# A sixteen-group, four-layer pipeline: order strings for all engines, a bank table, and step vectors with stationary weights

## The reference

```
x = x + L0(_gn(x))   # routed 1x1, 3x3, 1x1 convolutions; weights mixed from 8 experts per sample
x = x + L1(_gn(x))   # in-projection, depthwise conv, selective scan over permuted tokens, out-projection
x = x + L2(_gn(x))   # 1x1, 3x3 offsets, deformable 3x3, 1x1
x = x + L3(_gn(x))   # three convolutions, each squared (y + 1)^2, with batch norm
```

```
x_h = _gather_last(xf, perm)                    # tokens in the order of a permutation per head
dbc = einsum('oc,bcn->bon', dbc_w, xf) + dbc_b  # "step vectors": dt, B, C per head and token
dt = softplus(dbc[:, :, 0])
h = exp(dt*A) * h + (dt*B) * x ; y = C . h + D*x  # scan over the 196 tokens
y = _gather_last(y, inverse of perm)
```

## Time and profile before

| | us |
|---|---|
| median of three runs (1036.54 to 1048.52) | 1043.89 |
| the profiled execution | 1048.19 |
| its span, first to last instruction | 1046.0 |
| TensorE busy | 935.8 |
| VectorE busy | 731.9 |
| ScalarE busy | 550.1 |
| GpSimd busy | 362.4 |

### The profile page before, as it was taken

The page is one execution under the profiler, slowest core; times in us unless marked ns, Lnnn a source line. Parts: engine busy times, 40 slices in busy tenths (PEclk is TensorE's granted clock), DMA queues, the critical chain, the costliest instruction groups (busy, mean ns, idle before and its releaser), DMA issues.

```text
span 1046.0 us, 19785 instructions
## 1 busy us (share of the span) xinstructions
PE 935.8 (89%) x7460; PEld 635.9 (61%) x7460; DVE 731.9 (70%) x2047; ACT 550.1 (53%) x1155; POOL 362.4 (35%) x320
## 2 busy tenths in 40 slices
PE   3788988999999899999999999999999998887766
PEld 2555656666666566666666666666666665646454
DVE  2567377786878587878878687878787868756332
ACT  1143353756556474748475655657474747361412
POOL 3013433435251625344342525152524343342200
PEclk9889999999999999999999999999999999889998
DMA  9101153352626253544536262626353444426060
GB/s 220 37 8 44 40 141 121 85 177 75 184 75 178 70 169 108 145 128 116 161 94 188 76 190 72 182 79 168 96 164 113 128 130 118 147 64 189 15 207 16
DMA packets 116547, 123.33 MB, mean 118 GB/s; under 512 B 64802, under 2 KB 99750, under 8 KB 116454
## 3 DMA queue, kind: packets, MB, share of 16 engines
q1 hardware_dynamic: 107812, 105.45, 34.6%
q0 software_dynamic: 6144, 13.71, 4.6%
q10 hardware_dynamic: 2498, 2.91, 1.2%
HBM read 84.31 MB, written 37.73 MB: 117 GB/s over the span
## 4 chain that ended last, share of the span: by engine, by line
PE 30%; DVE 24%; issue 17%; POOL 13%; ACT 9%; DMA 5%; SPq 1%; ACTq 0%; POOLq 0%; DVEq 0%
PE ps L625 27%; DVE c_w L1301 4%; ACT y L986 3%; POOL rs L1215 3%; POOL b_ex L1215 3%; POOL b_cr L1215 2%; POOL b_yp L1263 2%; ACT L986 2%; POOL b_res L1215 2%; DVE y L1306 2%; DVE x L1309 2%; DVE st L1336 2%; DMA b_yp<-y_turned,b_to 2%; DVE b_xf L1309 1%; DVE y L1309 1%
## 5 line engine op out<-in xcount | busy, mean ns | idle before, releaser
L1263 POOL DMA_INDIRECT b_yp<-y_turned,b_to x64 | 90.3, 1411 | 271.5 <-DMA y_turned<-b_yt 256.9
L625 PE MATMUL ps<-y,inw 128*128 128x392 f32 x384 | 140.2, 509 | 1.3 <-DVE y L1306 1.3
L1215 POOL TENSOR_TENSOR rs<-ve,root 128x4 f32<-128x4 f32 x64 | 66.1, 1032 | 200.9 <-DVE ve L1305 200.4
L1336 DVE BATCH_NORM_STATS2 st<-x 128x6 f32<-128x196 f32 x256 | 73.7, 350 | 88.0 <-POOL x L1215 76.0
L1301 DVE TENSOR_TENSOR c_w<-c_w,c_hat 126x1176 f32<-126x1176 f32 (+1 forms) x64 | 97.8, 1580 | 11.2 <-DMA c_w<-hat_turned 11.2
L625 PE MATMUL ps<-c_w,c_zt 126*64 126x196 f32 x896 | 88.7, 345 | 11.6 <-DVE c_w L1301 6.9
L625 PEld LDWEIGHTS ps<-y,inw 128*128 128x128 f32 x384 | 70.6, 194 | 46.4 <-issue 6.8
L625 PE MATMUL ps<-w,a_S 128*32 128x384 f32 (+2 forms) x1280 | 81.6, 392 | 7.5 <-DVE a_S L1309 5.7
L625 PE MATMUL ps<-c 128*128 128x256 f32 (+1 forms) x284 | 86.7, 442 | 0.0
L986 ACT ACT_TABLE_LOAD x50 | 64.2, 1283 | 37.5 <-PE ps L625 36.7
L625 PEld LDWEIGHTS ps<-c_w,c_zt 126*64 126x64 f32 x896 | 63.8, 142 | 31.8 <-issue 14.3
(11 more groups left out here) (203 smaller groups left out, 2025.3 us busy)
## 6 DMA issues: line engine op xcount, KB each, us to landing
c_w<-hat_turned SPq DMA_DIRECT2D x32, 771.8 KB
c_w<-hat_turned SPq DMA_DIRECT2D x32, 578.8 KB
z_turned<-c_z SPq DMA_DIRECT2D x32, 441.0 KB
c_zt<-z_turned SPq DMA_DIRECT2D x16, 882.0 KB
b_xp<-x_turned SPq DMA_DIRECT2D x32, 222.0 KB
x<-in_x SPq DMA_DIRECT2D x32, 196.0 KB, 2.7
y_turned<-b_yt SPq DMA_DIRECT2D x32, 196.0 KB
out<-x SPq DMA_DIRECT2D x32, 196.0 KB, 7.3
```

The costliest lines, as they stand in the source:

```text
L625: return nc.tensor.matmul(o, l, r, start=start, stop=stop)
L1215: return nc.gpsimd.tensor_tensor(out=o, in0=x, in1=y, op=op)
L1263: nc.gpsimd.indirect_dma_start(out=YP[:, m, h].rearrange("p b d -> p (b d)"), out_offset=None, in_=y_dram[g % 2], in_offset=bass.IndirectO ...
L1336: last = nc.vector.bn_stats(st[s][:, 2 * c + b, :], x[:, c, b, :])
```

## The change

1. **Order.** `PLAN` and `FROM` go. `ORDER` has a string per engine with a letter per step (`LETTERS` names the stages); the steps of a stage come in their own order. Period by period, the order of the steady loop on TensorE differs from the old one in where steps stand, and the first four and last three groups have orders of their own.
2. **SyncE.** Per period in the loop: the two stores of `c_hat`, the first two hat loads, the two stores of `c_z`, the two stores of `y`, the load of `c_zt`, the second two hat loads, the load of `x_turned`, the output. Before: stores of `c_hat`, stores of `c_z`, first two hat loads, `c_zt`, one second hat load, stores of `y`, the other one, output, `x_turned`. The second pair of inputs is loaded ahead of the constants.
3. **Banks.** `BANKS` names the bank of each take; every step takes its bank ahead of its waits for data.
4. **Fillers.** `keep_busy` goes. `BUSY` gives the number of 128-column products (`group` times `group`) put between the wait for the bank and the wait for data: 7 ahead of `c1` and 4 ahead of `off` in groups 3 to 12, 13 and 4 in group 13, and 348 others in 48 places of the first six and last four groups, 14 of them ahead of the first routing product.
5. **Step vectors.** `dbcw` (34 columns, padded to 64) are the weights and `b_xf` streams, 196 columns a product. ScalarE adds the bias in the eviction to `b_row`, TensorE transposes `b_row` in two halves, VectorE evicts both into `XT`. The transposes of `b_xf` are taken for both samples in one bank, evicted by ScalarE (first token half) and VectorE (second). `b_bc`, `xq` as a tensor and its addition go; `xq` is a view of the reloaded block. Two small parameter loads are added (`dbcb`).

```diff
-        self.turn[f, g] = len(self.turn)
+        bank = int(self.banks[len(self.turn)])
+        self.turn[f, g] = bank, self.uses[bank]
+        self.uses[bank] += 1
...
+        ("off", 12): 4, ("c1", 13): 13, ("n1", 15): 3, ("off", 13): 4, ("n3", 12): 5, ("d2", 12): 6,
+        (("pt", 0), 14): 14, (("pt", 1), 14): 12, ("d1", 13): 7, (("pt", 0), 15): 5, (("pt", 1), 15): 3,
+        (("out", 0), 15): 6, ("n2", 15): 16, ("acc", 14): 2, ("off", 15): 9, ("n3", 14): 13,
+        ("d1", 14): 13, ("d2", 14): 7, ("acc", 15): 3, ("n3", 15): 13, ("d1", 15): 13, ("d2", 15): 7}
...
+LETTERS = "acbstuofgdhkz"
+ORDER = {
+    "tensor": (
...
+        "uussscktttddtkocoackoodddddfcdgcgcgcguguuuuuucggggggbcuchsssuussscktttddtkocoackoodddddfcdgcgcgcgugu"
...
+    "sync": (
+        "kaggddgguudddttkaggddgguudddttkaggddgguudddttkaggddgguudddttkaggddgguudddttkaggddgguudddttkggddgguud"
...
+BANKS = (
+        "0123456021345602134560213456021345602134560231456032145601435260143526014352601435206153240513420634"
...
+    return [next(todo[letter]) for letter in ORDER[name]]
...
+                t = ring.tile(f, g)
+                for _ in range(BUSY.get((f, g), 0)):
+                    mm(t[:, 0:128], k128("group"), k128("group"))
+                return t
...
-            def keep_busy(f, g, n):
-
-                t = take(f, g)
-                if first(g):
-                    pe.wait_ge(ld_c, 16 * 2)
-                lo = at128["expand"][0]
-                for _ in range(n):
-                    mm(t[:, 0:2 * N], ident, c128[:, lo:lo + 2 * N])
-
-            def take_early(f, g, ring=R):
-
-
-                t = take(f, g, ring)
-                for _ in range(BUSY.get((f, g), 0)):
-                    mm(t[:, 0:256], ident, c128[:, 0:256])
...
-                k, tt, b = part, part // G, part % G
-                if k == 0:
-                    pe.wait_ge(b_xf_ok.sem, b_xf_ok.count(g))
+                if i == 0:
+                    tt = part
+                    t = take(("xt", tt), g)
+                    if tt == 0:
+                        pe.wait_ge(b_xf_ok.sem, b_xf_ok.count(g))
+                        if first(g):
+                            pe.wait_ge(ld_c, 16 * 2)
+                    for h in range(HEADS):
+                        for b in range(G):
+                            last = nc.tensor.transpose(t[0:HT, (h * G + b) * HD:(h * G + b + 1) * HD],
+                                                       b_xf[:, h, b, tt * HT:(tt + 1) * HT], ident)
+                    last.then_inc(R.filled(("xt", tt), g), 1)
+                if i == 1:
                     if first(g):
-                        pe.wait_ge(ld_c, 16 * 2)
-                t = take(("xt", k), g)
-                cols = slice(tt * HT, (tt + 1) * HT)
-                for h in range(HEADS):
-                    nc.tensor.transpose(t[0:HT, h * XD:h * XD + HD], b_xf[:, h, b, cols], ident)
-                o = t[0:HT, 0:HEADS * XD].rearrange("p (h x) -> p h x", h=HEADS)[:, :, HD:XD]
-                for c in range(CC):
-                    last = mm(o, b_xf[:, c, b, cols], dbcw[:, c, :, :], start=(c == 0), stop=(c == CC - 1))
-                last.then_inc(R.filled(("xt", k), g), 1)
+                        pe.wait_ge(zeros, NZERO)
+                    t = take("db", g)
+                    for c in range(CC):
+                        for b in range(G):
+                            last = mm(t[half(b), 0:N], dbcw[:, c, :], b_xf[:, c, b, :], start=(c == 0), stop=(c == CC - 1))
+                    last.then_inc(R.filled("db", g), 1)
+                if i == 3:
+                    t = take("rows", g)
+                    drained(pe, "db", g)
+                    for tt in range(2):
+                        last = nc.tensor.transpose(t[0:HT, tt * 128:(tt + 1) * 128], b_row[:, tt * HT:(tt + 1) * HT], ident)
+                    last.then_inc(R.filled("rows", g), 1)
...
-                    keep_busy("c1", g, 1)
                 if i == 1:
...
-                if i == 2 and part == 0:
-                    keep_busy("off", g, 2)
-                if i == 2 and part == 1:
+                if i == 2:
+                    take("off", g)
...
+                if i == 0:
+                    if g:
+                        act.wait_ge(*x_out.at(g - 1))
+                    filled(act, ("xt", 0), g)
+                    fn(XT[:, 0, :, :, 0:HD].rearrange("p h b x -> p (h b) x"), R.tile(("xt", 0), g)[0:HT, :]
+                       .rearrange("p (q x) -> p q x", x=HD), ACT.Copy).then_inc(R.drained(("xt", 0), g), 1)
+                if i == 2:
+                    if first(g):
+                        act.wait_ge(ld_d, 16 * 13)
+                    filled(act, "db", g)
+                    fn(b_row[:, :], R.tile("db", g)[:, 0:N], ACT.Identity, bias=dbcb[:, 0:1])\
+                        .then_inc(R.drained("db", g), 1)
...
-                        pool.wait_ge(b_xq_ok.sem, b_xq_ok.count(g))
+                        pool.wait_ge(*x_back.at(g))
...
-                    tt(xq[:, :, :], XP[:, :, :, :, HD:XD].rearrange("p t h b x -> p (t h b) x"), b_bc[:, :, :], ALU.add)\
-                        .then_inc(b_xq_ok.sem, 1)
+                    filled(v, "rows", g)
+                    for tt in range(2):
+                        last = copy(XT[:, tt, :, :, HD:XD], R.tile("rows", g)[0:HT, tt * 128:(tt + 1) * 128]
+                                    .rearrange("p (b r) -> p b r", b=G)[:, :, 0:HEADS * DBC]
+                                    .rearrange("p b (h x) -> p h b x", h=HEADS))
+                    last.then_inc(R.drained("rows", g), 1)
...
-                    for t, name in ((inw, "inw"), (cvec, "cvec"), (dbcw, "dbcw"), (outw, "outw")):
+                    for t, name in ((inw, "inw"), (cvec, "cvec"), (outw, "outw")):
                         load(t[:], a[name], ld_s)
+                    load(dbcw[:, :, 0:HEADS * DBC], a["dbcw"].rearrange("p c h x -> p c (h x)"), ld_s)
```

More of the change, by code:

```diff
@@ L327, in planned @@
 def planned(name):
-    todo = []
-    for s, stage in enumerate(STAGES):
-        at = -1
-        for g in range(1 if stage == "once" else GROUPS):
-            for (i, part), start in zip(places(name, stage), PLAN[name][s], strict=True):
-                at = max(start + FROM[stage][g], at + 1)
-                todo.append((at, s, g, i, part))
-    return sorted(todo)
+    todo = {}
+    for letter, stage in zip(LETTERS, STAGES, strict=True):
+        todo[letter] = iter([(stage, g, i, part) for g in range(1 if stage == "once" else GROUPS)
+                             for i, part in places(name, stage)])
+    return [next(todo[letter]) for letter in ORDER[name]]
 def for_groups(name, steps):
-    for _, s, g, i, part in planned(name):
-        steps[STAGES[s]](i, part, g)
+    for stage, g, i, part in planned(name):
+        steps[stage](i, part, g)
 def first(g):
@@ L697, in c0 @@
                 if i == 2:
+                    t = take("w1", g)
                     pe.wait_ge(a_S_ok.sem, a_S_ok.count(g, 1))
@@ L719, in c0 @@
                     b = part
+                    t = take(("w2", b), g)
                     if b == 0:
@@ L794, in tb @@
                     b = part
+                    t = take(("re", b), g)
                     if b == 0:
@@ L806, in tb @@
                     k = part
+                    t = take(("same", k), g)
                     if k == 0:
@@ L810, in tb @@
                             pe.wait_ge(ld_c, 16 * 2)
-                    t = take(("same", k), g)
                     mm(t[0:HT, 0:448], k98("same"), CD[:, 4 * k:4 * k + 4].rearrange("p q s t -> p (q s t)"))\
@@ L836, in tb @@
                     tt = part
+                    t = take(("yt", tt), g)
                     if tt == 0:
@@ L852, in o1 @@
                     h = part
-                    take_early(("pt", h), g)
+                    take(("pt", h), g)
                     pe.wait_ge(*y_back[h].at(g))
@@ L862, in o1 @@
                     m = part
+                    t = take(("out", m), g)
                     if m == 0:
                         pe.wait_ge(b_y2.sem, b_y2.count(g))
-                    t = take(("out", m), g)
                     for c in range(CC):
@@ L932, in k3 @@
                         pe.wait_ge(folded, 1)
-                    take_early("d1", g)
+                    take("d1", g)
                     t = R.tile("d1", g)
@@ L936, in k3 @@
                 if i == 2:
-                    take_early("d2", g)
+                    take("d2", g)
                     drained(pe, "d1", g)
@@ L1234, in ta @@
                 if h == 0:
-                    for b in range(G):
-                        drained(pool, ("xt", 2 * m + b), g)
+                    drained(pool, ("xt", m), g)
+                    if m == 0:
+                        drained(pool, "rows", g)
                 nc.gpsimd.indirect_dma_start(
@@ L1493, in tb @@
                     m = part
+                    if m == 0 and first(g):
+                        v.wait_ge(tables, 1)
```

(2 more changed lines are left out.)

252 lines of the change are left out of this document (88 added, 164 removed), and 15 rows, old and new, of tables (BUSY, PARTS).

## The result

The changed kernel takes 1085.18 us (1082.25 to 1091.85), the kernel before 1044.1 beside it: 1.041 times as long, with a 95% interval of 1.033 to 1.049. It is slower by 41 us; the forecast was 1018 us, and 1044 the end of its range. The profiled execution has a span of 1082.8 us against 1046.0.

The account below looks back on a forecast made before the run. TensorE was taken to bound the loop, with 2.25 us idle a period and 84 us at the ends. Filling -10, loop -4 and draining -12 gave -26 from 1043.9: 1018 us, range 995 to 1044.

Parts of the forecast that it names:

- the order in the steady loop: Ten loop periods: new order leaves TensorE 1.9 us idle instead of 2.25; -4 us in all, bounds -22 and +12.
- The hand trace: Steady loop's new order followed with old durations: VectorE 5.0 us between `n2`'s statistics and `a_md`, TensorE waiting 0.9.
- Rival 3: Nothing measurable: gains at the ends lost in the loop and to clock falls; about 1042 us, chance 0.15.
- The price of 4 us a fall: Cost of one fall of TensorE's clock, from an old loop period of 59.90 us against 55.90.
- Rival 4: Loop slower: `z` load behind the store of `y` stops TensorE at `c_w`; about 1057 to 1073 us, chance 0.12.
- Rival 2: Loop closes up too, TensorE's order leaving no idle, a further 18 us: 1000 us, chance 0.18.
- Step vectors: Each group: TensorE gains 0.05 us, nothing; added latency 1.2 us, hidden in the loop, on the path in the last group.
- banks: Taking banks ahead of data waits: worth 0, bounds 0 and 0.8 us a period.
- Fillers: TensorE in groups 3 to 12: eleven short products, 2.6 us against 2.5; no gain, +0.1 a period.
- Filling: Start, before 253.9 us: 10 us gained of 41 idle, bounds 0 and 18.
- draining: End, last groups: less work ahead of the last scan; -12 us, bounds 0 and -25.
- The in-projection's 5.6 us: Draining: group 15's in-projection starts after 11.4 us instead of 17.2, bringing the last transposes 5.6 us forward.

Follow-up runs that it names:

- later_k3: Changed kernel with VectorE's two `k3` sums moved from ahead of `n2`'s statistics to behind those of `n1`, groups 2 to 11: 1094.25 us, 1.053.
- pow_after: Changed kernel with GpSimd's three wide jobs replaced by four-column powers of nearly the same length, work left out: 1057.15 us, 1.011.
- add_before: Kernel before with one GpSimd add of 98x784 put into its idle time in groups 2 to 13: 1067.82 us, 1.021.
- old_order: Changed kernel with the order of before on all five engines and banks in turn; step vectors, early takes, new fillers stay: 1097.17 us, 1.054.
- pool_x_first: Changed kernel with the order of before for GpSimd's adds and scatters alone, groups 3 to 12: 1137.16 us, 1.084.

## Why the prediction was wrong

**The step that failed is the order in the steady loop.** It was to give 4 us, with +12 as its worst bound; it cost 44 in the profiled executions. The bounds followed from durations of the old timeline, as if an instruction took its length along to its new place. Before, these instructions met no GpSimd instruction that hindered them, and the lengths in the earlier trace rows hold there. The new order put `d_o` beside the adds of `x`, `ms` beside those of `b_res` and `x<-y,bn_n,x` beside `b_cr`. The hand trace had 5.0 us between `n2`'s statistics and `a_md`; in the profile after, `st` ends near 790.8 and `a_md` starts at 797.6. 1.3 us of that is the stretched pair, and the statistics start 2.4 late behind `d_o`. The wait for `a_md` I put at 0.9 is 1.72 in that period, and the largest wait is not `a_md` but `n2`'s statistics, 2.69; over the ten periods they are 1.1 and 2.4 on average, 0.21 and 0.25 before.

I also followed one chain only. GpSimd's line, four scatters and then the adds of `x`, is as long as VectorE's, and later_k3 shows that it takes over at once. That the lengthened instructions are part of the cause is shown (pow_after, add_before); how the rest of the 41 us divides between GpSimd's line, the clock and the other places that moved stays open.

**Rival 3** named the clock, as something the ends would lose. It fell in the loop instead, to 0.96: TensorE is busy 55.5 us a period against 53.8, and it came with the order: in old_order, with the same fillers in the loop, the clock is 1.00. The price of 4 us a fall did not hold everywhere: in add_before a period with a mean clock of 0.97 takes 58.1 us and one of 0.94 59.8, against 57.0 at 1.00. **Rival 4**, the only slower one, had the wrong mechanism: VectorE's waits for hats (1.75 us in that period) come in four periods of ten, and SyncE's old order makes them worse. **Rival 2** did not occur.

**Step vectors, banks.** At nothing in TensorE's time, right in the main: busy 53.85 us a period in old_order against 53.62, both at full clock, where step vectors and fillers together were to add 0.05. But the added latency was said to be hidden in the loop, and in later_k3 it heads the chain that sets the period. **Fillers**, right in the loop. I had not priced them at the ends, where they are worth 25 us when they stand at the wrong waits.

**Filling and draining**, -10 and -12: measured -3.1 and -4.5. What I had named as signs came in part: the `w2` product takes 2.79 us instead of 4.52, and the last scan's first product comes 28.3 us after the last transposes, where I had said about 25 and it was 33.3. (The in-projection's 5.6 us in that sum should have been 5.8, 17.2 - 11.4.) Group 3's `a_md` does come 10.5 us earlier (129.0 for 139.5), but the next period takes 71.2 us instead of 58.1. I had counted idle time saved up to a group's mark as time saved, without asking which later stage's work had been left out of it. That this is what happened between groups 3 and 4 is how I read the two numbers; no run tests it.

**Range and chances.** With both chains and the meetings left out, "slower" had 0.10. A term that was called the weakest and was worked out over five engines should have had wider bounds than +12.

## What to carry to other kernels

An instruction's length belongs to its neighbours as well: before reordering VectorE or GpSimd, lay their two timelines over each other and see which instructions with all operands in SBUF meet newly, in both directions. In a loop in which several chains are within a microsecond or two of each other, taking one stall away can give nothing (later_k3), and moving steps of one or two engines out of an order that was made for all of them made the changed kernel slower in seven trials of seven, by 9 us (near the noise) to 67. The gain of an end counts only from a mark behind which both kernels have the same work left.

## What the runs showed of the hardware that was not expected

A VectorE instruction on four columns (`ms`) waited 1.16 us for GpSimd adds of 392 columns, so a short one waits as well as a long one. In later_k3 it even starts 0.03 us ahead of the first of two adds and ends after both:

```profile
478.66 2.05 DVE L1263 TENSOR_TENSOR ms<-gm 128x4 f32<-128x4 f32 x1
478.69 1.98 POOL L1176 TENSOR_TENSOR b_res<-b_res,b_gate 128x392 f32<-128x392 f32 x2
```

In add_before two VectorE instructions with two inputs in SBUF that start while the add runs (`b_xf` at 462.45, `d_o` at 462.99) keep their 0.62 us, and only the third waits: the profile's start times don't tell who will wait. Nor is it only instructions with two tensors as input: in pool_x_first VectorE's `y<-x,gm,rs`, with one tensor, took 1.27 us for 0.37 beside `b_cr`, in all ten periods. GpSimd's scatters stretched from 0.97 to between 1.4 and 2.5 us beside VectorE's `c_w`, its powers from 1.0 to 1.78 beside `b_adt` products, so the hindrance goes both ways. GpSimd powers on four columns, 1.0 us long, did not hold up VectorE's pair (1.16 beside 2.68 us of them).
